# Index lists of gathers and scatters copied once per two chunks instead of once per chunk, on one core

## What is computed

```python
h = relu(layernorm(x)); x = x + L0_gat(h, edge_index, ...)
h = relu(layernorm(x)); x = x + L1_gatv2(h, edge_index, edge_attr_16, ...)
h = relu(layernorm(x)); x = x + L2_attention(h, edge_index, edge_attr_18, ...)
h = relu(layernorm(x)); x = x + L3_rgcn_gru(h, edge_weight, src, dst, edge_type_3)
# inside L3, for each of 2 rounds:
t = einsum('nd,rde->rne', output, weight)
swh = segment_sum(t[rel_type, src] * norm[:, None], dst)
hstate = gru_cell(swh, hstate, ...)
```

## Time and profile before

| | |
|---|---|
| median of three runs | 8856.25 us |
| the profiled execution, its device time | 8784.2 us |
| its span, first to last instruction | 8782.3 us |
| `conv_gat`, GpSimd's first copy to its last scatter | 737 to 2141 us |
| `conv_gatv2` | 2145 to 3600 us |
| `conv_rpe` | 4286 to 6065 us |
| `conv_rgcn` l3a | 6072 to 7265 us |
| `conv_rgcn` l3b | 7274 to 8480 us |

### The profile page before, as it was taken

One profiled execution on the slowest core, in us unless ns is written; L12 is line 12 of the kernel. 1 busy time (PEld: TensorE's weight loads), 2 busy tenths in 40 slices (PEclk: granted clock), 3 DMA queues, 4 the chain that ended last, 5 costly groups with the idle time before them and its releaser, 6 DMA issues. The chain is left out here.

```text
span 8782.3 us, 75502 instructions
## 1 busy us (share of the span) xinstructions
PE 4269.5 (49%) x11974; PEld 2124.2 (24%) x11974; DVE 5410.8 (62%) x9130; ACT 2377.9 (27%) x4661; POOL 5878.3 (67%) x6277
## 2 busy tenths in 40 slices
PE   0002444443666666200266666665666666767740
PEld 0001111111222222000134434443333333333320
DVE  6854777775777777797166666665333335555554
ACT  1112333333333333332133333332111112222210
POOL 5875666665566665687677777775666666666665
PEclk9999999999666666555555555555666667777765
DMA  2332222222333333575111111111111121111149
GB/s 81 102 96 83 80 83 80 83 84 80 91 95 90 91 94 91 152 212 157 19 41 42 41 42 42 42 42 39 52 52 52 52 52 40 41 41 41 41 110 263
DMA packets 873137, 682.12 MB, mean 78 GB/s; under 512 B 663969, under 2 KB 697566, under 8 KB 872879
## 3 DMA queue, kind: packets, MB, share of 16 engines
q1 hardware_dynamic: 705463, 488.34, 19.6%
q0 software_dynamic: 163104, 167.63, 8.2%
q10 hardware_dynamic: 4512, 25.60, 1.0%
HBM read 385.09 MB, written 312.41 MB: 79 GB/s over the span
## 5 line engine op out<-in xcount | busy, mean ns | idle before, releaser
L728 POOL DMA_INDIRECT l_rows<-x,l_num x1176 | 1186.4, 1009 | 460.4 <-issue 373.0
L753 POOL DMA_INDIRECT o<-l_out,l_snum x392 | 407.8, 1040 | 391.4 <-DVEq L1228 284.2
L1330 POOL DMA_INDIRECT er_edge_rows<-eat,all_perm x392 | 531.6, 1356 | 145.0 <-issue 134.1
L753 POOL DMA_INDIRECT x<-l_out,l_snum x392 | 414.9, 1059 | 303.0 <-DVEq L1082 197.0
L728 POOL DMA_INDIRECT l_rows<-in_x,l_num x392 | 444.6, 1134 | 169.5 <-issue 158.2
L753 POOL DMA_INDIRECT xh<-l_out,l_snum x392 | 395.1, 1008 | 223.4 <-issue 165.4
L753 POOL DMA_INDIRECT g<-l3a_out,l3a_snum x392 | 402.2, 1026 | 200.8 <-issue 170.7
L753 POOL DMA_INDIRECT g<-l3b_out,l3b_snum x392 | 399.5, 1019 | 204.1 <-issue 177.4
L728 POOL DMA_INDIRECT l3b_rows<-g,l3b_num x392 | 388.7, 992 | 170.0 <-issue 102.7
L728 POOL DMA_INDIRECT l3a_rows<-xh,l3a_num x392 | 379.5, 968 | 169.6 <-issue 159.1
L936 POOL DMA_INDIRECT pre_src_rows<-in_x,all_idx_src x392 | 388.3, 991 | 140.8 <-issue 126.0
(11 more groups left out here) (366 smaller groups left out, 12763.4 us busy)
## 6 DMA issues: line engine op xcount, KB each, us to landing
l_far<-far_d SPq DMA_DIRECT2D x196, 256.0 KB
g<-l_fill SPq DMA_DIRECT2D x194, 256.0 KB
l_far<-far_s SPq DMA_DIRECT2D x98, 256.0 KB
o<-l_fill_o SPq DMA_DIRECT2D x97, 256.0 KB
xh<-l_fill_h SPq DMA_DIRECT2D x97, 256.0 KB
ts_xin<-in_x SPq DMA_DIRECT2D x31, 800.0 KB
x<-ts_row SPq DMA_DIRECT2D x31, 800.0 KB
d_xin<-x SPq DMA_DIRECT2D x31, 800.0 KB, 4.5
```

Source lines behind the costliest of these rows:

```text
L728: pool.indirect_dma_start(self.buf[k.u][:, j, at:at + w], None, table, bass.IndirectOffsetOnAxis(ap=self.num[k.u][:, m, j:j + 1], axis=0)) ...
L753: pool.indirect_dma_start(self.table, bass.IndirectOffsetOnAxis(ap=self.num[k.u][:, j:j + 1], axis=0), self.out[k.u][:, j, 0:self.cols], N ...
L1330: pool.indirect_dma_start(c.edge_rows[:, t, :], None, eat, bass.IndirectOffsetOnAxis(ap=c.perm[:, t:t + 1], axis=0)).then_inc(c.edges_gath ...
```

## The change

The copies of index columns move from each gather and each scatter to the start of a turn. `Rows.columns` copies the 8 columns of both chunks' gathers into a tile `num[v]` of double width, `Scatter.columns` the 8 columns of the two scatters of the turn into `snum[v]`, and v alternates by turn. GpSimd then waits once for `snum_ready` and once for `num_ready`. The gathers and scatters that follow keep their order and their waits for `rows_free`, `scattered` and `out_ready`, and no longer copy. As v has to be a constant in the code, the hardware loop now holds two turns a pass (turns 4 to 47); turns 0 to 3 and 48 to 50 are written out. Nothing changes on the other engines.

```diff
-    def gather(self, pool, k):
+    def columns(self, pool, t, v):
+        for m, (_, _, _, lst) in enumerate(self.lists):
+            pool.tensor_copy(self.num[v][:, m, :], lst[:, bass.ds(t * (2 * TPC), 2 * TPC)]).then_inc(self.num_ready, 1)
+
+    def gather(self, pool, k, v):
         if not k.first:
             hold(pool, self.rows_free, k.n - 2)
-        for m, (_, _, _, lst) in enumerate(self.lists):
-            pool.tensor_copy(self.num[k.u][:, m, :], lst[:, bass.ds(k.i * TPC, TPC)]).then_inc(self.num_ready, 1)
-        hold(pool, self.num_ready, k.n * len(self.lists))
...
-    def scatter(self, pool, k):
+    def columns(self, pool, t, lag, halves, v):
+        lo, n = halves[0] * TPC, len(halves) * TPC
+        pool.tensor_copy(self.num[v][:, lo:lo + n], self.lst[:, bass.ds((2 * t + halves[0] - lag) * TPC, n)]).then_inc(self.snum_ready, 1)
+
+    def scatter(self, pool, k, half, v):
         if not k.first:
             hold(pool, self.scattered[k.u], 16 * TPC * k.t)
-        pool.tensor_copy(self.num[k.u][:], self.lst[:, bass.ds(k.i * TPC, TPC)]).then_inc(self.snum_ready, 1)
-        hold(pool, self.snum_ready, k.n)
         hold(pool, self.out_ready, k.n)
...
+    def turn(t, v):
...
+        if gathers:
+            rows.columns(pool, t, v)
+        if halves:
+            sct.columns(pool, t, lag, halves, v)
+            hold(pool, sct.snum_ready, t - begin + 1)
+        if gathers:
+            hold(pool, rows.num_ready, (t + 1) * len(rows.lists))
+        for u in range(2):
+            if gathers:
+                rows.gather(pool, Chunk(t, u, c.NCH), v)
+            if u in halves:
+                sct.scatter(pool, Chunk(t - (lag + 1 - u) // 2, (u + lag) % 2, c.NCH), u, v)
...
+    with pool.Fori(head // 2, tail // 2) as q:
+        turn(2 * q, 0)
+        turn(2 * q + 1, 1)
```

More of the change, by code:

```diff
@@ L713, in __init__ @@
         self.buf = [s.sb(f"rows{u}", [P, TPC, width]) for u in range(2)]
-        self.num = [s.sb(f"num{u}", [P, len(lists), TPC], I32) for u in range(2)]
+        self.num = [s.sb(f"num{v}", [P, len(lists), 2 * TPC], I32) for v in range(2)]
         self.gathered = [s.swdge_sem(f"gathered{u}") for u in range(2)]
@@ L718, in __init__ @@
         self.per = 16 * TPC * len(lists)
-    def gather(self, pool, k):
+    def columns(self, pool, t, v):
+        for m, (_, _, _, lst) in enumerate(self.lists):
+            pool.tensor_copy(self.num[v][:, m, :], lst[:, bass.ds(t * (2 * TPC), 2 * TPC)]).then_inc(self.num_ready, 1)
+    def gather(self, pool, k, v):
         if not k.first:
             hold(pool, self.rows_free, k.n - 2)
-        for m, (_, _, _, lst) in enumerate(self.lists):
-            pool.tensor_copy(self.num[k.u][:, m, :], lst[:, bass.ds(k.i * TPC, TPC)]).then_inc(self.num_ready, 1)
-        hold(pool, self.num_ready, k.n * len(self.lists))
         for m, (table, w, at, _) in enumerate(self.lists):
             for j in range(TPC):
+                col = k.u * TPC + j
                 pool.indirect_dma_start(self.buf[k.u][:, j, at:at + w], None, table,
-                                        bass.IndirectOffsetOnAxis(ap=self.num[k.u][:, m, j:j + 1], axis=0)
+                                        bass.IndirectOffsetOnAxis(ap=self.num[v][:, m, col:col + 1], axis=0)
                                         ).then_inc(self.gathered[k.u], 16)
@@ L740, in __init__ @@
         self.table, self.lst, self.rows, self.cols = table, lst, rows, cols or width
-        self.num = [s.sb(f"snum{u}", [P, TPC], I32) for u in range(2)]
+        self.num = [s.sb(f"snum{v}", [P, 2 * TPC], I32) for v in range(2)]
         self.out = [s.sb(f"out{u}", [P, TPC, width]) for u in range(2)]
@@ L744, in __init__ @@
         self.snum_ready, self.out_ready = s.sem("snum_ready"), s.sem("out_ready")
-    def scatter(self, pool, k):
+    def columns(self, pool, t, lag, halves, v):
+        lo, n = halves[0] * TPC, len(halves) * TPC
+        pool.tensor_copy(self.num[v][:, lo:lo + n], self.lst[:, bass.ds((2 * t + halves[0] - lag) * TPC, n)]).then_inc(self.snum_ready, 1)
+    def scatter(self, pool, k, half, v):
         if not k.first:
             hold(pool, self.scattered[k.u], 16 * TPC * k.t)
-        pool.tensor_copy(self.num[k.u][:], self.lst[:, bass.ds(k.i * TPC, TPC)]).then_inc(self.snum_ready, 1)
-        hold(pool, self.snum_ready, k.n)
         hold(pool, self.out_ready, k.n)
-        for j in range(TPC):
-            pool.indirect_dma_start(self.table, bass.IndirectOffsetOnAxis(ap=self.num[k.u][:, j:j + 1], axis=0),
-                                    self.out[k.u][:, j, 0:self.cols], None, bounds_check=self.rows - 1, oob_is_err=False
+        for j in range(half * TPC, (half + 1) * TPC):
+            pool.indirect_dma_start(self.table, bass.IndirectOffsetOnAxis(ap=self.num[v][:, j:j + 1], axis=0),
+                                    self.out[k.u][:, j % TPC, 0:self.cols], None, bounds_check=self.rows - 1, oob_is_err=False
                                     ).then_inc(self.scattered[k.u], 16)
@@ L766, in gather_scatter @@
 def gather_scatter(pool, c, rows, sct, lag):
[L768 to L773, removed]
+    begin = lag // 2
+    def turn(t, v):
+        known = isinstance(t, int)
+        gathers = not known or t < c.TURNS
+        halves = [u for u in range(2) if sct and (not known or 0 <= 2 * t + u - lag < c.NCH)]
+        if gathers:
[10 more added lines that the diff above has]
+                sct.scatter(pool, Chunk(t - (lag + 1 - u) // 2, (u + lag) % 2, c.NCH), u, v)
+    head, tail = 4, c.TURNS - 1
+    assert head >= begin + 2 and tail % 2 == 0
+    for t in range(head):
+        turn(t, t % 2)
+    with pool.Fori(head // 2, tail // 2) as q:
+        turn(2 * q, 0)
+        turn(2 * q + 1, 1)
+    for t in range(tail, c.TURNS + (begin + 1 if sct else 0)):
+        turn(t, t % 2)
     if sct:
```

## The result

The changed kernel took 9080.19 us (median of 4 runs, 9051.71 to 9113.5) beside 8855.58 us of the kernel before (4 runs, 8849.47 to 8865.16), a ratio of 1.0254, 95% interval 1.0215 to 1.0293. I had forecast 8666 us, faster.

What follows compares the result with a forecast made beforehand. GpSimd's own instruction train was taken to bound l3a and mostly l3b, VectorE's chain l0 to l2. Gains of 100 and 90 us gave 8594 us profiled; plus 72 us, 8666 us, range 8614 to 8730.

Steps and rivals of the forecast that it cites:

- The three mid-turn places cost 0.30 us: GpSimd's train starts without a copy, three a turn, cost 0.30 us each; bounds 0.30 to 0.95.
- Rival (a): Mid-turn waits of GpSimd are not free, 0.82 to 0.95 us each; only 30 us gained, 8826 us; 6%.
- A turn's start costs 1.30 us: GpSimd's two copies and three waits ahead of a turn's first gather take 1.30 us; bounds 1.16 to 1.42.
- l3a -100, l3b -90: Gains in us in the two stages that GpSimd paces; about a tenth of l3b's taken as lost to VectorE.
- The sum for GpSimd's starts: Starts in l3a and l3b fall from 4.34 to 2.20 us a turn, saving 102.6 us a stage.
- feared them doubled: Unexplained 2.11 us gaps in trains, seven in l3a; coming twice as often, they would lose 25 us over two stages.
- The others keep up, at 9.56 and 10.81 us a chunk: Other engines' pace in l3a and l3b, below the 10.94 and 11.04 us that GpSimd will need.
- l0, l1 and l2: nothing: No gain in these stages, where VectorE's chain sets the pace and GpSimd's saving turns into waits.
- The sign that I gave for it: In l0, l1 and l2, lengths within 5 us, GpSimd's waits for VectorE grown by about 50 us a stage or more.
- VectorE's waits for rows near 190 and 70 us: Expected remaining waits of VectorE for gathered rows in l3a and l3b, from 288.6 and 159.1 us before.
- Rival (d): Slower: shifted GpSimd work holds up VectorE in l0, l1 and l2; at 1.0 us a chunk 8960 us; 4%.
- 72 us between the runs and the profiled run: Kernel before: median run 8856.25 us, profiled 8784.2; the same difference was added to the forecast.

Runs made afterwards that it cites:

- e5: The changed kernel, nothing edited, run again with the kernel before timed on the same chip: 8534.1 us, 0.9742 of the kernel before.
- e6: The kernel before, nothing edited, run again for its trace: 8759.3 us, 0.9997 of the kernel before.
- e9: The changed kernel with ScalarE held back by eight extra activations on each turn's first chunk in the l3a and l3b loops: 8942.2 us, 1.0212 of the kernel before.
- e3: The changed kernel with three copies and their waits a turn put back between the trains in l3a and l3b: 8814.2 us, 1.0064 of the kernel before.
- e4: The changed kernel with three added copies and waits, all at the start of each turn in l3a and l3b: 8622.2 us, 0.9846 of the kernel before.
- e8: The changed kernel with GpSimd's program written out in l3a and l3b, indices taken from the lists without copies: 8416.9 us, 0.9611 of the kernel before.
- e14: The changed kernel with one mid-turn copy and its wait put back in l3a and l3b: 8618.9 us, 0.9851 of the kernel before.
- e7: The changed kernel, nothing edited, on another chip: 8525.7 us, 0.9736 of the kernel before.
- e10: The changed kernel, nothing edited, on another chip: 8528.2 us, 0.9741 of the kernel before.
- e12: The changed kernel, nothing edited, on a fifth chip: 8532.3 us, 0.9751 of the kernel before.

## Why the prediction was wrong

I take its steps in order, first against the runs in which updates arrive in time, then against the first result.

**The three mid-turn places cost 0.30 us.** Right, on both sides: in e5 the medians of the gaps from gather to scatter and from scatter to gather are 0.30 us in l3a and in l3b. Rival (a) is out.

**A turn's start costs 1.30 us.** In the median 1.41 in the first result and in e5 alike (1.43 in e5's turn at 6515.86 us, 1.27 to 1.29 in some that are written out). At the upper bound of 1.42, and worth 5 us a stage.

**l3a -100, l3b -90.** e5 against e6: -119.6 and -109.0. The sum for GpSimd's starts holds (47 x (4.34 - 2.31) = 95 us). What I had not counted: the gaps of 2.1 us inside the scatters' trains, seven in each stage in e6 as in the earlier trace rows, are gone in e5, all of them (12.6 us a stage), where I had feared them doubled; and l3a's scatters take 999 ns on average and not 1027 (11 us). I don't know the cause of either. It is not the missing copies alone: the seven gaps are there in the first result and in e9, whose GpSimd program is the changed one, and in e3, and not in e4, e8 and e14.

**The others keep up, at 9.56 and 10.81 us a chunk.** In l3b I took 10.81 for what VectorE can do and counted a tenth of the gain as lost. e8's l3b runs at 10.49. The figure came from the first chunks, and was no limit.

**l0, l1 and l2: nothing.** Right where updates are in time: l2's first scatter at 4351.2 against 4351.6, its length 1685.5 against 1684.9. The sign that I gave for it, GpSimd's waits for VectorE grown by 50 us a stage, came in l0 (195.9 to 280.9 us) and l2 (36.4 to 122.7) and not in l1 (284.5 to 278.5), though l1 kept its length. **VectorE's waits for rows near 190 and 70 us**: 183.9 and 71.0.

In ratio I had 8666 / 8856 = 0.979; these chips give 0.974.

**The step that failed** for the result as it was measured is one that I never wrote down as a step: that the chain behind VectorE passes its signals on as fast with GpSimd's pauses gone as with them. "The others keep up" was read from rows with pauses in GpSimd's train. Where the first result was taken, TensorE's update for about every second chunk of l3a and l3b reached its semaphore late, 2.1 to 13.6 us after the last transposes in l3a and up to 16.2 in l3b, and ScalarE, TensorE's next matmuls, VectorE and in the end GpSimd stood behind it: a chunk took 12.75 us in l3a and 13.95 in l3b, not the 9.56 and 10.81 that I had given the others. Rival (d), slower through VectorE in l0 to l2, had the sign and not the mechanism: nothing was lost in l0 and l1, and the 37 us in l2 go with late updates of TensorE. My 4% for slower was far too little, with two warnings in my own hands: 72 us between the runs and the profiled run, which I carried along as a constant, and waits of ScalarE for TensorE in l2's head with releasers that could not be true.

**What stays open.** Why updates were late then and on none of five chips since, and what decides where they are late. The traces tie them to GpSimd's train, in three ways. At 21 of the 23 odd chunks of l3a from 5 to 49, none late, GpSimd had run for at most 1.6 us since a wait of 1.5 to 9.1 us, and at the other two (15 and 41) for about 6 since the turn's start; at the late even chunks up to 48 it had run for 7.7 us or more. The 13 updates of `turned` that took over 12 us all came while GpSimd stood still, 11 of them 1.8 to 2.6 us after its last gather had ended, as in the rows above (7545.73, and ScalarE at 7547.74); that it has run out of work by then is no wonder, that the update follows so regularly is. And the three late odd chunks of l3b (29, 55, 81) are 26 chunks apart, as are the four longest of l3a (16, 42, 68, 94): 208 of GpSimd's DMAs, twice the 104 from one 2.1 us gap to the next. This speaks for theory 2, that a running train holds TensorE's updates up, but it is a pattern in one trace, and the train is not enough: in e5 it runs for 18 us and more ahead of most odd chunks without a late update. Nor is it the missing copies that are needed: the kernel before has its pauses of 0.8 to 1.1 us twice a chunk in l2 as in l3, and had late updates in l2. It could not be tried, because no run of this study had a late update. ScalarE's loop is out, by the semaphore's own record. By the Trainium skill (Runtime: NRT & Kernel Launch, section "Instruction fetch mechanics") a taken branch out of the fetched window costs a fetch; the trace doesn't bear it out as the cause here, since ScalarE started 0.02 us after the update. Of the records of semaphore changes 38% and 50% are missing from the first traces of before and of the changed kernel (82 and 66 thousand are there, against 132 thousand in e6, e7 and e10); whether that has the same cause is not known.

## What to carry to other kernels

Where GpSimd's train sets the pace, group its copies so that their waits stand behind one another and only the last stands before an indirect DMA (0.974 where updates were in time); better still, give the indirect DMA its indices in place (0.961, with GpSimd's program written out). Before a forecast, look whether a wait's named releaser can raise that semaphore at all, and whether profiled and other runs agree: if not, something outside the program may be part of the time, and a change should be timed again on another chip before it is judged. To tell a late signal from a late waiter, compare the recorded moment of the semaphore's change with the start of the engine that waited.

## What the runs showed of the hardware

- TensorE's semaphore update lies 0.29 to 0.44 us after the start of the last transpose (e5, e7, e12); in the first result it took up to 16.2 us, on about every second chunk, with nothing in TensorE's own rows to show it, and other updates of TensorE were late too.
- A wait for GpSimd's own copy costs 0.13 to 0.26 us of idle ahead of another copy (e4) and 0.82 to 1.08 us ahead of an indirect DMA.
- An extra 143 GB/s of transfers into SBUF beside 800 us of gathers and scatters cost 14 us on the whole program (8543 against 8528).
- Lateness of 5 us of ScalarE once a turn came out at 0.83 to 0.92 of its size (e9): l3a and l3b have hardly any slack once GpSimd's pauses are gone.
